# Four residual layers on one core: fc1's high products first, the second half of the pooling weights behind the first normalisation, and the fourth weighing and the pooling ahead of the second layer's row products

## The reference, cut to what matters

```python
x = x + pooled(x)        # layer 0: masked softmax pooling over the 32 tokens of a row
x = x + attention(x)     # layer 1: 16 heads of 8, scores with a bias per token and row, softmax, output projection
x = x + lora_ffn(x)      # layer 2: relu(x @ wi + expert part) @ wo + expert part, one of 8 experts per row
x = x + gelu_ffn(x)      # layer 3: gelu(x @ fc1 + b) @ [fc2 | expert's fc2], one of 16 experts per row
```

## Time and profile before

| | |
|---|---|
| median of 3 runs | 320.29 us (317.44 to 321.67) |
| the profiled execution | 318.7 us, its span 316.9 us, mean granted TensorE clock 0.935 |
| TensorE, matmuls | 270.8 us busy, 85% of the span |
| TensorE, weight loads | 193.8 us, 61% (they overlap the matmuls) |
| VectorE | 195.8 us, 62% |
| ScalarE | 130.5 us, 41% |
| GpSimd | 116.5 us, 37% |
| chain of waits | TensorE 40%, issue 23%, VectorE 11%, GpSimd 9% |
| PEclk in 40 slices | 9999955556999999999999999999999999999979 |

### The profile page before, as it was taken

The page is one execution under the profiler, slowest core; times in us unless marked ns, Lnnn a source line. Parts: engine busy times, 40 slices in busy tenths (PEclk is TensorE's granted clock), DMA queues, the critical chain, the costliest instruction groups (busy, mean ns, idle before and its releaser), DMA issues.

```text
span 316.9 us, 12449 instructions
## 1 busy us (share of the span) xinstructions
PE 270.8 (85%) x4794; PEld 193.8 (61%) x4794; DVE 195.8 (62%) x369; ACT 130.5 (41%) x220; POOL 116.5 (37%) x229
## 2 busy tenths in 40 slices
PE   0348899999879998899989998999998999978865
PEld 0134654445647776676767685867585777757744
DVE  3288670253985877778676958794878576563030
ACT  1033422021263735365534554374636374632231
POOL 6040246003245335524550455054424534660420
PEclk9999955556999999999999999999999999999979
DMA  6405860001550454055205512550354352065000
GB/s 167 177 2 172 252 177 0 0 2 61 219 189 4 141 206 160 2 199 199 99 6 225 199 66 68 203 226 0 116 203 177 143 217 76 9 229 199 5 0 35
DMA packets 26749, 38.25 MB, mean 121 GB/s; under 512 B 10577, under 2 KB 10833, under 8 KB 26594
## 3 DMA queue, kind: packets, MB, share of 16 engines
q1 hardware_dynamic: 26722, 37.87, 34.0%
HBM read 10.60 MB, written 2.10 MB: 40 GB/s over the span
## 4 chain that ended last, share of the span: by engine, by line
PE 40%; issue 23%; DVE 11%; POOL 9%; POOLq 9%; ACT 4%; DMA 3%; SPq 1%; DVEq 0%; ACTq 0%
PE pB L682 8%; POOLq L328 5%; PE pB L715 5%; PE pB L710 5%; POOL sc L310 4%; PE pB L742 4%; POOLq L338 3%; DMA rwo<-rank_w_dram 3%; PE pV L626 2%; PE pB L640 2%; PE pB L636 2%; POOL x3b L318 2%; PE pA L579 2%; POOL rw L329 2%; PE pB L637 2%
## 5 line engine op out<-in xcount | busy, mean ns | idle before, releaser
L310 POOL TENSOR_TENSOR sc<-sc,rmax 128x512 f32<-128x512 f32 x32 | 33.6, 1050 | 84.0 <-DVE rmax L1007 83.9
L329 POOL COPY rw<-e3t_s 128x128 f32 x128 | 37.4, 293 | 52.7 <-issue 45.7
L439 ACT ACTIVATE ex<-sc 128x512 f32<-128x512 f32 x32 | 20.2, 630 | 43.7 <-POOL sc L310 43.3
L339 POOL COPY rwo<-weff 128x512 f32 x32 | 21.5, 678 | 31.9 <-ACT weff L461 22.6
L1013 DVE STREAM_TRANSPOSE pt<-ex 128x512 f32<-128x512 f32 x32 | 22.7, 708 | 16.4 <-ACT ex L439 16.2
L742 PE MATMUL pB<-rw,hT 128*32 128x128 f32 x1024 | 32.1, 274 | 0.6 <-ACT hT L447 0.4
L682 PE MATMUL pB<-rwo,hT 128*32 128x128 f32 x1024 | 29.7, 273 | 1.0 <-ACT hT L443 1.0
L742 PEld LDWEIGHTS pB<-rw,hT 128*32 128x32 f32 x1024 | 27.2, 110 | 3.2 <-issue 2.6
L1002 DVE SCALAR_TENSOR_TENSOR sc<-pS,bias 128x512 f32<-128x512 f32 x32 | 21.5, 672 | 12.4 <-PE pS L611 12.4
L640 PE MATMUL pB<-x_l,ffn_h 128*128 128x512 f32 x56 | 23.3, 416 | 6.4 <-DVE x_l L1060 5.8
L682 PEld LDWEIGHTS pB<-rwo,hT 128*32 128x32 f32 x1024 | 27.7, 110 | 1.5 <-ACT hT L443 1.5
(11 more groups left out here) (133 smaller groups left out, 506.1 us busy)
## 6 DMA issues: line engine op xcount, KB each, us to landing
rwo<-weff SPq DMA_DIRECT2D x96, 256.0 KB, 2.3
rw<-fc2t_dram SPq DMA_DIRECT2D x4, 768.0 KB, 8.8
xT<-xt_dram SPq DMA_DIRECT2D x8, 256.0 KB, 2.6
xN<-xn_dram SPq DMA_DIRECT2D x8, 256.0 KB, 2.9
out_dram<-o_s SPq DMA_DIRECT2D x8, 256.0 KB, 2.3
e3t_s<-e3t_dram SPq DMA_DIRECT2D x1, 1024.0 KB, 7.4
rwo<-ffn_w_dram SPq DMA_DIRECT2D x1, 896.0 KB, 6.5
rwo<-ffn_w_dram SPq DMA_DIRECT2D x1, 512.0 KB, 11.7
```

The costliest lines, as they stand in the source:

```text
L310: pool.tensor_tensor(sc[:, g % 2, :, :], sc[:, g % 2, :, :], rmax[:, g % 2, :].unsqueeze(2).to_broadcast([P, H, S]), ALU.subtract).then_in ...
L329: pool.tensor_copy(rw[:, r, :, SHARED:D], e3t_s[:, bass.ds(e, 1), :, :].rearrange("p o c n -> p (o c) n"))\
L339: pool.tensor_copy(rwo[:, row, :, :].rearrange("p c d -> p (c d)"), weff[:, bass.ds(e, 1), :, :].rearrange("p o c d -> p (o c d)")).then_i ...
```

## The change

Three orders are changed, and no computation.

- fc1 of a block: the function issues the first two products (both by the high part of x3) of chunks 0, 1 and 2, then waits once for the low part of x3, issues the three third products, each counting its chunk, and does chunk 3 as before. Before, each chunk was finished before the next was begun. This holds in every step and in the tail.
- TensorE's order in a step: `weigh(n, 3)` and `pooling(n + 1)` come before `out_rows(n - 1)` and no longer behind it.
- VectorE's order in a step: `pool_weights(n + 1, 1)` comes behind `normalise(n, 0)` and no longer in front of `turn(n, 0)`. Step 7 has neither pooling nor pooling weights.

```diff
--- before.py
+++ after.py
@@ -716,13 +716,19 @@
                               bpair[k, :, :], start=False, stop=(c == 1))
                 last.then_inc(weff_ps, 1)
 
-            def fc1(i, c):
-                if c == 0:
-                    at(pe, x3_sb, 2 * (i + 1))
-                if c == 2:
-
-                    at(pe, sc_sb, G * NBLK if isinstance(i, int) and i == NBLK - 1 else G * (i + 2))
-                parts3(GIN[c][:, :], weight(N_FC1, c), whole(x3p), True, True, (x3l_sb, i + 1)).then_inc(g_ps, 1)
+            def fc1(i):
+
+                at(pe, x3_sb, 2 * (i + 1))
+                for c in range(FC - 1):
+                    if c == 2:
+                        at(pe, sc_sb, G * NBLK if isinstance(i, int) and i == NBLK - 1 else G * (i + 2))
+                    high, low_part = weight(N_FC1, c)
+                    mm(GIN[c][:, :], high, x3p[0][:, :], start=True, stop=False)
+                    mm(GIN[c][:, :], low_part, x3p[0][:, :], start=False, stop=False)
+                at(pe, x3l_sb, i + 1)
+                for c in range(FC - 1):
+                    mm(GIN[c][:, :], weight(N_FC1, c)[0], x3p[1][:, :], start=False, stop=True).then_inc(g_ps, 1)
+                parts3(GIN[FC - 1][:, :], weight(N_FC1, FC - 1), whole(x3p), True, True).then_inc(g_ps, 1)
 
             def token_major(i):
                 at(pe, x3b_sb, i + 1)
@@ -835,14 +841,13 @@
                 hidden(n - 1, 3)
                 hidden_expert(n - 1, 3)
                 weigh(n, 2)
-                out_rows(n - 1)
                 weigh(n, 3)
                 if next_block:
                     pooling(n + 1)
+                out_rows(n - 1)
                 out_turn(n - 1)
                 attn_out(n)
-                for c in range(FC):
-                    fc1(n - 1, c)
+                fc1(n - 1)
 
             step_of(1, None)
             with pe.Fori(2, NBLK - 1) as n:
@@ -857,8 +862,7 @@
                 hidden_expert(NBLK - 1, c)
             out_rows(NBLK - 1)
             out_turn(NBLK - 1)
-            for c in range(FC):
-                fc1(NBLK - 1, c)
+            fc1(NBLK - 1)
             token_major(NBLK - 1)
             for g in range(G):
                 final(NBLK - 1, g)
@@ -1110,14 +1114,14 @@
                 score_max(n, 1)
                 if last is not None:
                     result(last)
-                if next_block:
-                    pool_weights(n + 1, 1)
                 turn(n, 0)
                 score_max(n, 2)
                 turn(n, 1)
                 score_max(n, 3)
                 turn(n, 2)
                 normalise(n, 0)
+                if next_block:
+                    pool_weights(n + 1, 1)
                 turn(n, 3)
                 normalise(n, 1)
                 x3(n - 1)
```

## The result

The changed kernel takes 344.15 us in the median of four runs (341.76 to 347.01), the kernel before 319.18 (317.44 to 321.67) beside it. The ratio is 1.075, with a 95% interval of 1.063 to 1.087: slower.

A forecast was written before the change was run, and what follows sets the result against it. TensorE's queue was taken to set the period. +2.42 us a block over six steps (14.4), +0.5 for the seventh and -1.0 in the tail give +13.9; with 6.4 for the clock, 318.7 becomes 339.0 us, range 328 to 347.

The forecast's parts named there:

- the second cover: Weighing and pooling no longer lie over ScalarE's copy of outn, so the transposes of outn wait: 0.93 us a block.
- the clock's: TensorE's clock falls to 1.2 GHz behind the gap in four of six blocks, 1.6 us each: 6.4 us (0 to 9.5).
- third weighing earlier: With VectorE's pooling weights moved later, TensorE's third weighing starts at 123.6 in the block: 1.10 us earlier.
- the gap, with the 0.05: TensorE stands 3.10 us (2.85 to 3.9) before the fourth weighing; the third weighing holds it 0.05 us longer.
- `low` to queries: The third product of `low` waits for the low part of x2: about 0.28 us new a block.
- The shared port: VectorE's line 976 beside GpSimd's fourth subtraction: mutual blocking by the skill's rule, up to 0.7 us; rule not used in the sum.
- The +0.5 for the seventh step: Step without pooling weights: the same terms with a gap of some 1.7 us, +0.5 us.
- The tail: Behind the last step, fc1's gain alone applies: about -1.0 us.
- without the clock's fall: Rival: the gap opens but the clock stays at 2.4 GHz; 329 to 337 us, most likely 332.6; chance 0.27.
- the clock did not stay down for good: Rival: small products behind the gap run at 1.2 GHz for several stretches; 350 to 365 us; chance 0.06.
- the gap did open: Answers the no-gap rival: fourth transpose ready when the third weighing ends, block -0.68 us, 314 us; chance 0.04.
- the two gains did not cancel it: Answers the rival that the three edits cancel: fourth weighing starts at 125.5, 317 to 325 us; chance 0.05.

The follow-up runs named there:

- gap_filled: The whole change plus eight unused products between the third and fourth weighing: 334.9 us, ratio 1.049 to the kernel before.
- vector_and_fc1: The change with TensorE's order of before, so only VectorE's and fc1's edits: 310.0 us, ratio 0.968 to the kernel before.
- fc1_alone: The kernel before with only fc1's new order: 314.4 us, ratio 0.984.
- tensor_order_alone: The kernel before with only the fourth weighing and pooling moved ahead of the row products: 348.7 us, ratio 1.087.
- tensor_and_fc1: The whole change without VectorE's move of the pooling weights: 346.9 us, ratio 1.091 to the kernel before.
- gap_half_filled: The whole change plus four unused products between the third and fourth weighing: 342.7 us, ratio 1.073 to the kernel before.
- tensor_fc1_pooling_back: The change with pooling put back behind the row products and VectorE's order of before: 337.4 us, ratio 1.059 to the kernel before.
- pooling_back: The whole change with pooling put back behind the row products, the fourth weighing still ahead: 333.0 us, ratio 1.045 to the kernel before.
- late_weights: The change with pooling behind the row products and VectorE's pooling weights behind the fourth transpose: 322.3 us, ratio 1.013 to the kernel before.
- pool_weights_alone: The kernel before with only VectorE's pooling weights moved later: 312.5 us, ratio 0.977.

## Why the prediction was right

It named the time 339, the range 328 to 347 and the direction; 344.15 lies within. The mechanism was right too: the wait opened where it was said to and for the reason given, and the second cover went. One term was wrong, the clock's: the prediction's own last line says that it is wrong if PEclk falls in every block, and it fell in every block that has the gap in full. That the time is inside the range even so is owed to the range's width, which was laid over two cases; the clock's 10.7 us lie outside the bounds of their own term (0 to 9.5 us).

The sum of a block against the distances from start to start in steps 4 to 6, where they agree from step to step:

| term | predicted, us | measured, us |
|---|---|---|
| third weighing earlier (from the queries: 18.44 before, 17.19 after) | -1.10 | -1.25 |
| third weighing to the next work (0.36 before, 3.57 after): the gap, with the 0.05 | +3.15 | +3.21 |
| copy of outn (fourth weighing to transposes 5.90 in gap_filled; row products, weighing and pooling 4.92 before) | +0.93 | +0.98 |
| transposes to fc1 (1.86 before, 1.90 after): oT and x3 | +0.04 | +0.04 |
| fc1 (3.86 before, 2.94 after) | -0.88 | -0.92 |
| `low` to queries (0.69 before, 1.20 after) | +0.28 | +0.51 |
| sum, without the clock | +2.42 | +2.57 |

- *The gap.* Predicted 3.1 us (2.85 to 3.9); measured 3.06 to 3.36 in the six steps, and 1.55 in the seventh (predicted 1.7). Shown by taking the order back (310.0) and by taking it alone (348.7). The order's terms in the sum, 0.05 + 3.10 + 0.93 - 0.22 + 0.26 = 4.12 us a block, can be held against 33.0 (gap_filled) less 28.9 (vector_and_fc1) = 4.1, with some luck: the gap side is 0.3 us longer there than in the change, and vector_and_fc1 loses 0.4 us in front of its row products.
- *The shared port.* A product beside the subtraction was slowed, by 0.5 to 0.8 us. In steps 1 and 3 it was the one that the prediction had, line 976 then and 980 now (0.77 and 0.97 us), in the other four its neighbour, line 984. The prediction let only part of this into the sum. The rule of the Trainium skill, page "SBUF — State Buffer", section "Who interferes with whom", held: with two inputs in SBUF beside a GpSimd subtraction 0.90 us, away from it 0.29.
- *The mis-sized term of a block* was `low`: 0.28 us was the length of its wait, and the trace does mark 0.21 to 0.28 us of idle time, but from start to start it costs 0.51, in fc1_alone as well. The third weighing came 0.15 us better than predicted. Only in step 2 did it come 0.92 earlier and not 1.25: there GpSimd's third subtraction, which stands behind four copies, starts 14.1 us behind the queries (123.75) and not 13.7 as in step 4, and VectorE waits 0.22 us for the exponential that follows it.
- *The steps before the clock.* From the first queries to the seventh it is 282.73 - 76.76 = 205.97 us, 179.12 before: 26.85 more. Less the clock's 10.7 that is 16.2 us, with 6 x 2.4 = 14.4 predicted; steps 2 and 3, at +3.1 and +2.8, make most of the difference. The +0.5 for the seventh step is not what the listed terms give (with a gap of 1.7 us they make +1.0); about +0.6 was measured.
- *outn, fc1.* 0.73 us idle for outn (0.6 to 0.8 predicted), no wait left in fc1.
- *The clock.* "Four of six, at 1.6 us each" was the judgement it said it was, and too low: six of six, one of them long, 10.7 us and not 6.4. The 1.6 us of one fall was right (1.3 to 1.6, and 2.9 for the long one). In its argument the preparation's row PEclk stands at 5 for four slices, not five.
- *The whole.* The span grew by 24.6 us: 16.2 in the six steps, 10.7 by the clock, -1.0 because the first step began earlier, and -1.3 behind the seventh queries (-0.5 predicted). With 13.9 + 6.4 = 20.3 predicted, this leads from 339.0 to 343.3, the profiled execution.
- *The tail.* Predicted -1.0:

```profile
328.14 0.66 PE L689 MATMUL pB<-cols_s,lowm 128*128 128x128 f32 x4 [0.72 <-ACT lowm L452]
330.04 0.50 PE L726 MATMUL pB<-x_h,ffn_h 128*128 128x512 f32 x1 [1.24 <-DVE x_h L1062]
...
331.53 0.69 PE L730 MATMUL pB<-x_l,ffn_h 128*128 128x512 f32 x2
...
334.60 3.70 PE L748 MATMUL pB<-rw,hT 128*32 128x128 f32 x128 [1.01 <-ACT hT L447]
```

fc1 runs 2.95 us from its start to the next instruction's, with 308.97 - 303.54 = 5.43 before: the stall is gone, and the clock did not fall here. ScalarE's GELUs take 1.01 us of it back in front of the last products. From fc1 to those it is 4.56 us, and 6.46 before (310.00 on the row that follows): 1.9 us, not 1.0. In fc1_alone and vector_and_fc1, behind the same idle times of 0.72 and 1.24 us, the clock did fall, and there the tail gained 1.0 and 0.8 us. So the prediction had the stall right, and the rest is that the clock stayed up, which it had not considered.

The rivals: without the clock's fall the change would have been at 333 to 335, as gap_filled shows and as the rival had it; the clock did not stay down for good; the gap did open, and the two gains did not cancel it. The prediction didn't say that the other two edits alone would be worth 3%. Its terms for them, -1.10 and -0.60 a block, contained it: -1.7 together, with -1.25 measured, 0.4 of which is the new wait for hT.

## What to carry to other kernels

An instruction moved ahead on an in-order engine must be held against the time at which its operand comes; if the engine gets to it sooner than the operand comes, everything behind it waits, and whatever brings the engine there still earlier goes half or more into a longer gap, as VectorE's move did here. The long, independent work (here 3.5 us of row products) belongs in front of the instruction that is served last, and a move of work on another engine, as VectorE's here, was free as long as that cover stood. A gap of a few us on TensorE can cost more than its length, since the clock can fall behind it: here 1.3 to 1.7 us for each fall, and 2.9 for a long one.

## What the runs showed of the hardware that was not expected

All counts are of one execution of each kernel. They can differ between executions: the mean granted clock of the change was 0.915 in the profiled one and 0.899 and 0.895 in two others.

- The clock fell behind gaps of 1.7 to 2.6 us, in six of six steps each of tensor_order_alone, tensor_and_fc1, gap_half_filled and tensor_fc1_pooling_back. With 0.8 to 1.4 us left (gap_filled) it never fell, nor behind the 1.55 us of the seventh step (six kernels), nor behind the 1.65 to 1.67 us in front of the first weighing of the first step, before and in four others.
- At one length of the gap it can go either way: 3.1 to 3.4 us, six of six in the change; 2.7 to 3.4 us, four of six in pooling_back; 2.2 to 2.5 us, every time in those four kernels and one time in five in late_weights. late_weights had hardly any idle time ahead of the gap; tensor_fc1_pooling_back had 0.73 and 0.57 us within the ten us before, but gap_half_filled, where the clock fell every time with pooling behind the gap, had hardly more than late_weights. What decides was not settled.
- Falls for twice the usual time (some 7 us instead of 3.4) came in the loop only where pooling's products were the first dense work behind the gap: one in the change, two in tensor_and_fc1, two in tensor_order_alone, one in gap_half_filled; where the row products came first there was none among eleven falls. In the tails of pool_weights_alone and tensor_order_alone, where there is no pooling, the clock stayed down as long, over fc1's products. So pooling is not needed for it, and why is open.
